# The second FFN's rows of three batches, added by GpSimd's adding transfers in place of fetches and VectorE sums

## The chip, the cores and the metric

The kernel runs on one core of one Trainium2 chip. The metric is the device time of one execution in microseconds (us), the median of several runs. PE is TensorE, ACT is ScalarE, DVE is VectorE, POOL is GpSimd; SyncE issues most DMA transfers from its queue, SPq.

## What is computed

`x` has 4 batches of 512 tokens with 256 channels. Four layers are added to it in turn. The change touches how the result of the last one is added.

```python
x = x + attention_a(layernorm(x))      # 16 heads of 16, 4 key groups, causal
x = x + ffn(layernorm(x))              # 8 experts, the best 2 of each token
x = x + attention_b(layernorm(x))      # linear attention over 4 memory banks
x = x + ffn(layernorm(x))              # the same experts again

def ffn(x):
    probs = softmax(x @ Wr);  w, idx = top_k(probs, 2);  w = w / sum(w)
    y_e = (silu(x @ Wg[e]) * (x @ Wu[e])) @ Wd[e]
    return sum over the 2 chosen e of w_e * y_e
```

## The kernel before

`xall` [128, 16, 256] holds x in SBUF, four tiles of 128 tokens for each of the 4 batches (`b`), and every layer adds to it there. The two FFNs (`f` = 0 and 1) route each token to two experts. The normed rows are scattered by expert into `xs[f]` in HBM (`scatter`). The experts then work through 39 tiles (`TILES`) of 128 rows each; a tile is a pass of steps `load` (SyncE), `xT`, `gate_up`, `hidden`, `down` (TensorE, each followed by ScalarE or VectorE work) and a last `down` on GpSimd, an indirect DMA that scatters the weighted 128x256 results `yo` into `ys[f]` in HBM (L1876), two rows (k = 0, 1) for each token. The tiles are sorted so that those before number 31 (`MIXED`) have all rows of batches 0 to 2, and the last eight, 31 to 38, finish batch 3. VectorE writes `yo` in four buffers (`NYO` = 4): `down` of tile j there waits until the scatter of tile j - 4 has landed.

When the last four tiles that a batch needs have landed (27 to 30 for batches 0 to 2, 35 to 38 for batch 3), `combine` (L455) brings its rows back, in one of two ways.
- A batch in `JOINED` (L194) is fetched: for each half h, SyncE issues a `fetch` of two transfers (k = 0, 1) of 256 KB from `ys` into `fetched`, which lies in the memory of `kbd` (L913; the profile names it `kbd<-ys`), and VectorE does a `join`, two sums of 128x512 into `xall` (L1734, L1735). There are two buffers, so the third fetched batch of the list waits for the first one's joins.
- A batch that is not in it gets two steps `add` on GpSimd, k = 0 and 1 (L1870): each one transfer of 512 KB with `accum_op=ALU.add` that adds the k rows of the whole batch straight to `xall`. The k = 1 transfer waits on GpSimd until the k = 0 one has landed. Before the change these are batches 1 to 3 of the first FFN.

After that SyncE writes the batch out, two `store` steps of 256 KB (L919), and at the end waits for all eight.

**The order on the engines** is made when the program is built. `plan_work` (L516) lists each step with its engine, a rank, a planned duration, a planned time from issue to landing (`lands`), and what it waits for; `Work.order` (L141) goes through time and, for the step that can start first, lets a step of lower rank on that engine go ahead if it can start hardly later (`PATIENCE`). Each engine then issues its steps in exactly that order. Its planned numbers are the program's own and not measured. Ranks at the end are `last + 3j + 6` for `down` of tile j and `last + 78 + b` for `combine` of batch b. The planner's entries for the steps of `combine` and the stores are these.

```python
# combine, not in JOINED (k = 0, 1); rows: the last four scatters the batch needs
w.add(POOL, rank + 0.1 * k, 1.4, "add", f, b, k, after=rows + [(POOL, "add", f, b, 0)] * k,
      behind=[(POOL, "pow", 1, 0)], lands=8.0)
# in JOINED
w.add(SP, rank + 0.1 * k, 0.75, "fetch", f, b, k, after=rows + ([(DVE, "join", *JOINED[n - 2], 1)] if n >= 2 else [])
      + [(SP, "fetch", f, b, 0)] * k, lands=3.3)
w.add(DVE, rank, 1.34, "join", f, b, h, after=[(SP, "fetch", f, b, h)], behind=[(DVE, "join", f, b, 0)] * h)
```

Of the kernel before, what the change touches and what calls it, by code (L numbers as in the profile page):

```python
# [17 lines left out]
B, S, D = 4, 512, 256  # L18
# [28 lines left out]
TILES = 2 * B * S // P + NE - 1  # L47
# [143 lines left out]

JOINED = [(0, 0)] + [(1, b) for b in range(B)]  # L194


def tiles_with(b):
# [4 lines left out]
def spread(lo, hi, n):  # L202

    return iter([lo + (hi - lo) * (k + 0.5) / n for k in range(n)])


PE, ACTE, DVE, POOL, SP = "PE", "ACT", "DVE", "POOL", "SP"
# [130 lines left out]
def back(w, b, ranks):  # L338

    r = lambda: next(ranks)  # L340
    m = M_BANKS if b < B - 1 else TAIL_BANKS
    w.add(PE, r(), 0.45, "outT", b, after=[(DVE, "normalize", b, g) for g in range(NG)], banks=m, emptied=(ACTE, "outT", b))
    w.add(ACTE, r(), 0.92, "outT", b, after=[(PE, "outT", b)] + [(PE, "project", b - 1, 1)] * (b > 0))
    for n in range(2):
        w.add(PE, r(), 1.05, "project", b, n, after=[(ACTE, "outT", b), (ACTE, "out_weights")], behind=[(PE, "project", b, 0)] * n, banks=m,
              emptied=(DVE, "project", b, n))
        w.add(DVE, r(), 0.6, "project", b, n, after=[(PE, "project", b, n), (ACTE, "f_apply", b, 1)]
              + [(applies(b, NT - 1), "f_apply", b, NT - 1)])
# [9 lines left out]
def norm(w, s, b, ranks, banks):  # L358


    r = lambda: next(ranks)
    last = before(s, b)
    for n in range(2):
        src = ([(DVE, "project", b, n)], [(DVE, "join", 0, b, n) if (0, b) in JOINED else (POOL, "add", 0, b, 1)],
               [(DVE, "mem_out", b, 2 * n), (DVE, "mem_out", b, 2 * n + 1)])[s]
        w.add(DVE, r(), 1.15, "stats", s, b, n, after=src + ([(POOL, "pow", *last), (DVE, "scale", *last)] if last else []))
    w.add(POOL, r(), 1.03, "pow", s, b, after=[(DVE, "stats", s, b, n) for n in range(2)]
          + ([(ACTE, "apply", *last, NT - 1)] if last else []))
    w.add(DVE, r(), 0.1, "scale", s, b, after=[(POOL, "pow", s, b)] + ([(ACTE, "apply", *last, NT - 1)] if last else []))
    if s == 1:  # L370
        old = [(PE, "turn", 1, b - 1, kc) for kc in range(KC) if b]
    else:
        old = [(POOL, "scatter", s // 2, b - 2, i, k) for i in range(NT) for k in range(2)] if b >= 2 else []
        if s == 2 and b < 2:
            old = [(POOL, "scatter", 0, b + 2, i, k) for i in range(NT) for k in range(2)]
    for i in range(NT):
        w.add(ACTE, r(), 0.49, "apply", s, b, i, after=[(DVE, "scale", s, b)] + old
              + [(ACTE, "apply", s, b, i - 1)] * (i > 0))
    if s != 1:
        w.add(SP, r(), 0.5, "copy", s, b, after=[(ACTE, "apply", s, b, NT - 1)], lands=2.5)  # L380
    for kc in range(KC):
        w.add(PE, r(), 0.44, "turn", s, b, kc, after=[(ACTE, "apply", s, b, NT - 1)], behind=[(PE, "turn", s, b, 0)] * kc, banks=banks,
              emptied=(ACTE, "turn", s, b, kc))
        w.add(ACTE, r(), 0.5, "turn", s, b, kc, after=[(PE, "turn", s, b, kc)]
              + ([(PE, "mq", b - 1, mc) for mc in range(KC) if b] if s == 1 else
                 [(PE, "router", last[0] // 2, last[1])] if last else []))
# [68 lines left out]
def combine(w, f, b, rank):  # L455

    done = tiles_with(b)
    rows = [(POOL, "down", f, j) for j in range(done - NYO, done)]
    n = JOINED.index((f, b)) if (f, b) in JOINED else None
    for k in range(2):  # L460
# [3 lines left out]
        else:  # L464

            w.add(SP, rank + 0.1 * k, 0.75, "fetch", f, b, k, after=rows + ([(DVE, "join", *JOINED[n - 2], 1)] if n >= 2 else [])
                  + [(SP, "fetch", f, b, 0)] * k, lands=3.3)
# [48 lines left out]
def plan_work():  # L516
    w = Work()
    unit = lambda u: UNIT * u
    w.add(SP, -999, 1.2, "load_x", 0, lands=2.6)
    w.add(SP, -998, 0.5, "load_x", 1, behind=[(SP, "load_x", 0)], lands=2.8)  # L520
    w.add(SP, -997, 0.5, "constants", behind=[(SP, "load_x", 1)], lands=5.2)
    w.add(SP, -996, 4.0, "load_late", behind=[(SP, "constants")], lands=11.0)
    w.add(SP, unit(2), 2.0, "load_experts", behind=[(SP, "place_keys", 0, NG - 1)], lands=20.0)
    w.add(ACTE, -600, 0.8, "constants", after=[(SP, "constants")], behind=[(ACTE, "f_apply", 0, 1)])
    w.add(POOL, -700, 0.7, "bias", after=[(SP, "constants")])
    w.add(ACTE, unit(20), 0.8, "out_weights", after=[(SP, "constants")], behind=[(ACTE, "queriesT", 0, 2)])
    w.add(DVE, -999, 3.0, "presets")
    w.add(DVE, -800, 0.3, "constants", after=[(SP, "constants"), (DVE, "presets")])
    w.add(DVE, -500, 0.15, "scales", after=[(SP, "constants")])
    w.add(DVE, -300, 0.35, "masks", after=[(SP, "constants")])  # L530
    w.add(POOL, -999, 6.4, "presets")
    w.add(POOL, -500, 1.2, "constants", after=[(DVE, "scales"), (POOL, "presets")])
    w.add(POOL, unit(6), 1.7, "late", after=[(SP, "load_late"), (POOL, "constants")])
    for k, time in enumerate((0.5, 2.6)):
        w.add(DVE, unit(16), time, ("bank_shift", "banks")[k], after=[((SP, "load_late"), (ACTE, "banks"))[k],
                                                                      (DVE, "queries", 0, 1)])
    w.add(ACTE, unit(16), 0.3, "banks", after=[(DVE, "bank_shift")])
    w.add(SP, unit(8), 8.0, "spare", after=[(POOL, "late"), (SP, "load_experts")])
    tail = unit(BU * B)
    for b in range(B):  # L540
        lo = unit(BU * (b - 1) + 2)
        front(w, b, spread(-900, -100, 64) if b == 0 else spread(lo, unit(BU * b - 5), 64))
        scores(w, b, unit)
        t0 = unit(BU * (b + 1) + NU + 1 + LAG)
        t1 = unit(BU * (b + 1) + (26 if b == B - 2 else 36))
        if b == B - 1:
            t0, t1 = tail, tail + 1
        back(w, b, spread(t0, t0 + 0.3 * (t1 - t0), 8))
        m = M_BANKS if b < B - 1 else TAIL_BANKS
        norm(w, 0, b, spread(t0 + 0.3 * (t1 - t0), t0 + 0.7 * (t1 - t0), 16), m)  # L550
        route(w, 0, b, spread(t0 + 0.7 * (t1 - t0), t1, 16), m)
    release(w, 0, 0, unit(BU * B - 2), M_BANKS)
    release(w, 0, 1, unit(BU * B + 2), M_BANKS)
    release(w, 0, 2, tail + 2, TAIL_BANKS)
    for j in range(TILES):
        rank = tail + 20 + 3 * j + 8 * max(0, j - MIXED)
        rest = (1, 2) if j < LEAD else (2, 3, 4) if j < STAGES[LAST][1] else (2, 3, 4, 7)
        tile(w, 0, j, rank, 3, {"X": rest, "G": (0, 1)[:1 + (j >= LEAD)], "H": rest, "Y": rest})
    start = tail + 20 + 3 * MIXED
    for b in range(B):  # L560
        combine(w, 0, b, start - 20 + b)
        t = start + TURN * b
        memory(w, b, t - 18, t, t + TURN)
        norm(w, 2, b, spread(t + TURN, t + TURN + 6, 16), (7,))
        route(w, 1, b, spread(t + TURN + 6, t + TURN + 12, 16), (7,))
    last = start + TURN * (B + 1)
    for n, (batches, _, _) in enumerate(STAGES):
        release(w, 1, n, start + TURN * batches + 13, (7,))
    for j in range(TILES):
        rest = (3, 4, 5, 6) if j < STAGES[LAST][1] else (3, 4, 5, 6, 7)  # L570
        tile(w, 1, j, last + 3 * j, 3, {"X": rest, "G": (1, 2), "H": rest, "Y": rest})
    for b in range(B):
        combine(w, 1, b, last + 2 * TILES + b)
        for h in range(2):
            w.add(SP, last + 2 * TILES + b + 0.5, 0.4, "store", b, h, after=[(DVE, "join", 1, b, h)], lands=2.8)
    return w


ORDER, PLACE = plan_work().order()

FIRST_PACK = {"ident": (P,), "wqkv": (KC, QKV), "bqkv": (QKV,), "nscale": (2, 2, HD), "turns": (2, NT, HD), "mask": (P,)}
# [9 lines left out]
def build(nc, x, first_pack, late_pack, norm_sums, experts, out):  # L591
# [4 lines left out]
    with ExitStack() as ctx:  # L596
# [215 lines left out]
        def combined(eng, f, b, halves=2):  # L812

            if (f, b) in JOINED:
                eng.wait_ge(joined, 2 * JOINED.index((f, b)) + halves)
            else:
                eng.wait_ge(added[b], 16 * 2 * sum((g, b) not in JOINED for g in range(f + 1)))

# [1138 lines left out]
```

## Time and profile before

| | |
|---|---|
| median of 3 runs | 535.22 us (531.47 to 540.63) |
| the profiled execution, whole | 536.22 us |
| its span, first to last instruction | 534.4 us |
| PE busy | 483.7 us (91%) |
| DVE busy | 373.3 us (70%) |
| POOL busy | 248.5 us (46%) |
| DMA, mean over the span | 114 GB/s |
| SyncE's DMA queue (q1) | 38.24 MB, 23.0% of 16 engines' span |
| GpSimd's DMA queue (q0) | 21.83 MB, 13.6% |
| mean granted TensorE clock | 0.965 |

Busy shares are means over stages that differ. The span starts with the first attention. The first FFN's tiles (matmuls of L1138) begin at 187 us and end before 305, the second attention is mixed in and follows, and the second FFN's tiles run from 407.7 to 518 us. The last 16 us hold no matmul. Times below are us from the span's start.

### The profile page before, as it was taken

To read this page: it belongs to the slowest core of one execution; us is meant where nothing else is said; L and a number is where in the kernel's file an instruction comes from. 1 tells how busy PE (TensorE), PEld (TensorE's weight loads), DVE (VectorE), ACT (ScalarE), POOL (GpSimd) and SP (SyncE) were. 2 spreads that over 40 slices of the span, in tenths; PEclk is the share of its full clock that TensorE was granted. 3 is DMA by queue.
4 is the path that set the end of the run, shared out by engine and by line. 5 is a ranking of instruction groups with operands and counts; after the bars stand their busy time and mean duration, and the time that the engine had idled before them with its cause. 6 is when DMAs were issued, how large, how long until landed. Compare 5 with 4: busy or idle time off the path is not lost.

```text
span 534.4 us, 10902 instructions
## 1 busy us (share of the span) xinstructions
PE 483.7 (91%) x3346; PEld 327.6 (61%) x3346; DVE 373.3 (70%) x1098; ACT 269.3 (50%) x642; POOL 248.5 (46%) x308
## 2 busy tenths in 40 slices
PE   5799899999999999989999979999979998999960
PEld 2335555665665666766777636675757776677740
DVE  4799989879999966664445647868868684344473
ACT  3578898877887784423333425524223532334320
POOL 5408519338850062373433555446473756233330
PEclk8789999999999999999999999999989999799995
DMA  8254510111120232454335392102151457233484
GB/s 278 114 198 206 165 35 8 56 41 61 61 84 19 84 129 78 122 187 140 95 113 158 76 191 41 37 34 81 41 155 43 141 158 209 80 101 107 161 295 165
DMA packets 43736, 60.77 MB, mean 114 GB/s; under 512 B 5856, under 2 KB 38240, under 8 KB 43040
## 3 DMA queue, kind: packets, MB, share of 16 engines
q1 hardware_dynamic: 33696, 38.24, 23.0%
q0 software_dynamic: 9984, 21.83, 13.6%
q8 instruction: 29, 0.48, 0.4%
q14 instruction: 27, 0.22, 0.1%
HBM read 28.89 MB, written 25.00 MB: 101 GB/s over the span
## 4 chain that ended last, share of the span: by engine, by line
PE 58%; DVE 10%; DMA 5%; issue 4%; ACT 2%; POOL 2%; SPq 1%; POOLq 0%; DVEq 0%; ACTq 0%
PE PS L1138 15%; PE PS L1155 10%; PE PS L1184 4%; PE PS L1025 3%; PE PS L1119 3%; PE PS L1147 3%; PE PS L1002 3%; PE PS L1193 3%; PE PS L1087 2%; PE PS L1201 2%; DMA ys<-yo,xin 2%; DVE smax L1477 2%; PE PS L1165 2%; PE PS L1076 2%; DMA kbd<-ys 2%
## 5 line engine op out<-in xcount | busy, mean ns | idle before, releaser
L1876 POOL DMA_INDIRECT ys<-yo,xin x78 | 75.4, 966 | 107.3 <-DVE yo L1698 97.6
L1138 PE MATMUL PS<-wexp,xTt 128*128 x312 | 106.8, 470 | 2.2 <-issue 1.3
L1477 DVE TENSOR_REDUCE smax<-PS 128x1 f32<-128x512 f32 (+3 forms) x176 | 102.3, 633 | 6.1 <-PE PS L1004 5.6
L1303 ACT ACTIVATE prob<-PS 128x512 f16<-128x512 f32 (+1 forms) x176 | 92.7, 562 | 20.1 <-PE PS L1027 18.2
L1861 POOL DMA_INDIRECT xs<-xn,pos x64 | 62.5, 977 | 57.9 <-DVE pos L1572 40.8
L1155 PE MATMUL PS<-wexp,hT 88*128 x312 | 81.3, 388 | 2.3 <-ACT hT L1353 2.1
L1138 PEld LDWEIGHTS PS<-wexp,xTt 128*128 128x128 f32 x312 | 55.6, 192 | 25.1 <-issue 5.2
L1685 DVE SCALAR_TENSOR_TENSOR sg<-th,PS 128x176 f32<-128x176 f32 x78 | 26.2, 336 | 61.6 <-ACT th L1347 61.3
L1347 ACT ACTIVATE th<-PS 128x176 f32<-128x176 f32 x78 | 24.7, 317 | 83.9 <-PE PS L1138 83.9
L1155 PEld LDWEIGHTS PS<-wexp,hT 88*128 88x128 f32 x312 | 55.9, 191 | 15.2 <-issue 4.2
L1025 PE MATMUL PS<-qT,kbd 128*128 128x512 f16 (+3 forms) x256 | 60.8, 300 | 2.2 <-ACT qT L1295 1.0
L1002 PE MATMUL PS<-kbd,qT 128*128 128x512 f16 (+1 forms) x176 | 60.3, 367 | 2.4 <-DVE smax L1477 1.7
L1698 DVE TENSOR_SCALAR yo<-PS,xin 128x256 f32<-128x256 f32 x78 | 37.4, 482 | 26.3 <-PE PS L1155 22.6
L1353 ACT ACTIVATE hT<-PS 88x256 f32<-88x256 f32 x78 | 29.5, 378 | 40.2 <-PE PS L1147 39.3
L1004 PE MATMUL PS<-mask_b,ident_b 128*128 128x128 bf16 (+2 forms) x176 | 43.2, 245 | 0.0
L1027 PE MATMUL PS<-ident_b,mask_b 128*128 128x128 bf16 (+2 forms) x176 | 42.8, 243 | 0.0
L1043 PEld LDWEIGHTS PS<-vaug,prob 128*128 128x128 f16 x640 | 32.8, 96 | 16.1 <-ACT prob L1303 3.0
L1043 PE MATMUL PS<-vaug,prob 128*128 128x17 f16 x640 | 38.6, 172 | 1.5 <-ACT prob L1303 1.3
L1184 PE MATMUL PS<-late_rows,qT 128*128 128x512 f32 x64 | 33.3, 625 | 5.1 <-DVE qa L1724 4.7
L1883 POOL TENSOR_TENSOR qa<-qa 128x256 f32<-128x256 f32 x32 | 23.2, 756 | 23.5 <-DVE qa L1724 23.4
L1147 PE MATMUL PS<-first_rows,hf 128*88 128x128 f32 x156 | 30.2, 275 | 3.9 <-DVE hf L1689 3.6
L1341 ACT ACTIVATE xTt<-PS 128x256 f32<-128x256 f32 x78 | 26.4, 382 | 10.1 <-PE PS L1119 9.7
(210 smaller groups left out, 836.7 us busy)
## 6 DMA issues: line engine op xcount, KB each, us to landing
xin<-xs SPq DMA_DIRECT2D x78, 129.0 KB, 2.1
kbd<-ys SPq DMA_DIRECT2D x20, 256.0 KB, 4.3
wexp<-in_experts SPq DMA_DIRECT2D x4, 1216.0 KB, 9.1
xs<-zeros SPq DMA_DIRECT2D x32, 129.0 KB
xn<-xn SPq DMA_DIRECT2D x8, 512.0 KB, 3.3
xall<-ys POOLq DMA_DIRECT2D x6, 512.0 KB, 6.8
out<-xall SPq DMA_DIRECT2D x8, 256.0 KB, 2.7
kbd<-kT SPq DMA_DIRECT2D x60, 32.0 KB, 1.9
```

What stands on the lines that cost most here:

```text
L1002: pe.matmul(o, qT1[:, b % 2, g, i * P:(i + 1) * P], kbd[:, g, r0:r0 + nr, 0:w], start=True, stop=False, skip_group_check=True)
L1004: pe.matmul(o[:, :, i * P:w], ident_b[:], mask_b[:].unsqueeze(1).to_broadcast([P, nr, P]), start=False, stop=True, skip_group_check=True). ...
L1025: pe.matmul(o[:, k], kbd[:, g, r0 + k, j * P:(j + 1) * P], qT2[:, g % 2, j * P:S], start=(k == 0), stop=False, skip_group_check=True)
L1043: mm = pe.matmul(o[:, i, r0 + k], prob[:, u % NPR, k * w + (i - j) * P:k * w + (i - j + 1) * P], vaug[:, b, j, g], start=(n == 0 and k == ...
L1138: mm = pe.matmul(PS[:, bank, 0:2 * FI], xTt[:, j % NXT, kc * P:(kc + 1) * P], wexp[:, bass.ds(expert[f, j], 1), kc * 2 * FI:(kc + 1) * 2 * FI]
L1147: mm = pe.transpose(PS[0:FH, bank, c * P:(c + 1) * P], hf[:, j % 2, c * FH:(c + 1) * FH], ident_f)
L1155: mm = pe.matmul(PS[:, bank, 0:D], hT[:, j % 2, c * P:(c + 1) * P], wexp[0:FH, bass.ds(expert[f, j], 1), DOWN + c * D:DOWN + (c + 1) * D] ...
L1184: pe.matmul(PS[:, bank], sig[:, b % 2, kc, i * P:(i + 1) * P], late["mem"][:, kc], start=True, stop=True).then_inc(filled[bank], 1)
L1303: act.activation(prob[:, u % NPR, 0:nr * w], PS[:, bank, 0:nr * w], ACT.Exp, scale=ATT_SCALE)\
L1477: dve.tensor_reduce(smax[:, i, REP * g + r0:REP * g + r0 + nr], PS[:, bank, 0:nr * w].rearrange("p (r w) -> p r w", r=nr), AX.X, ALU.max). ...
L1861: pool.indirect_dma_start(xs[f], bass.IndirectOffsetOnAxis(pos[:, f, b, i, k:k + 1], axis=0), xn[:, b % 2, i, k], None).then_inc(scattered ...
L1876: pool.indirect_dma_start(ys[f], bass.IndirectOffsetOnAxis(xin[:, j % NXIN, D + 1:D + 2].bitcast(I32), axis=0), yo[:, j % NYO], None).then ...
```

## The change

The list `JOINED` loses batches 0, 1 and 2 of the second FFN. They are then added by GpSimd's transfers like batches 1 to 3 of the first. Batch 0 of the first FFN and batch 3 of the second stay fetched; batch 3 becomes the list's second, so it has a buffer of its own and no fetch waits for a join. The planner is told that a store of the three batches waits for the k = 1 add. `combined` (L812), `fetch`, `join` and `add` in the engines' programs read the same list and need no edit.

```diff
--- before.py
+++ after.py
@@ -191,7 +191,7 @@
 
 
 
-JOINED = [(0, 0)] + [(1, b) for b in range(B)]
+JOINED = [(0, 0), (1, B - 1)]
 
 
 def tiles_with(b):
@@ -572,7 +572,8 @@
     for b in range(B):
         combine(w, 1, b, last + 2 * TILES + b)
         for h in range(2):
-            w.add(SP, last + 2 * TILES + b + 0.5, 0.4, "store", b, h, after=[(DVE, "join", 1, b, h)], lands=2.8)
+            w.add(SP, last + 2 * TILES + b + 0.5, 0.4, "store", b, h, after=[(DVE, "join", 1, b, h) if (1, b) in JOINED else (POOL, "add", 1, b, 1)],
+                  lands=2.8)
     return w
```

## Rows read from the trace of the kernel before

**Rows 1.** The page: the span.

```profile
span 534.4 us, 10902 instructions
```

**Rows 2.** Chain of waits, 515 to 534 us: start, us, what.

```profile
519.18 4.25 DMA ys<-yo,xin
...
523.57 0.36 SPq L913
...
524.49 0.47 SPq L919
...
525.53 4.39 DMA kbd<-ys
...
529.95 0.70 DVE xall L1734
```

**Rows 3.** Timeline of SyncE's queue, 490 us on: start, us, queue, line, operation.

```profile
502.40 2.61 SPq L913 DMA_DIRECT2D kbd<-ys  x4
505.20 0.36 SPq L903 DMA_DIRECT2D xin<-xs  x1
505.73 1.94 SPq L913 DMA_DIRECT2D kbd<-ys  x4
```

**Rows 4.** Timeline of GpSimd, 490 us on: also idle before [releaser].

```profile
503.43 0.96 POOL L1876 DMA_INDIRECT ys<-yo,xin  x1 [0.30 <-issue]
...
519.18 0.96 POOL L1876 DMA_INDIRECT ys<-yo,xin  x1 [0.30 <-issue]
```

**Rows 5.** Timeline of VectorE, 490 us on.

```profile
510.97 0.48 DVE L1698 TENSOR_SCALAR yo<-PS,xin 128x256 f32<-128x256 f32 x1
...
514.64 0.48 DVE L1698 TENSOR_SCALAR yo<-PS,xin 128x256 f32<-128x256 f32 x1
...
517.93 0.48 DVE L1698 TENSOR_SCALAR yo<-PS,xin 128x256 f32<-128x256 f32 x1 [1.41 <-PE PS L1155]
```

**Rows 6.** Timeline of TensorE: `down` of tiles 34, 35 and 38.

```profile
506.90 1.13 PE L1155 MATMUL PS<-wexp,hT 88*128 x4
...
510.45 1.03 PE L1155 MATMUL PS<-wexp,hT 88*128 x4
...
516.77 1.12 PE L1155 MATMUL PS<-wexp,hT 88*128 x4 [0.56 <-ACT hT L1353]
```

**Rows 7.** Timeline of GpSimd, 300 to 315 us (first FFN's adds).

```profile
301.63 2.75 POOL L1870 DMA_DIRECT2D xall<-ys  x2
304.68 1.09 POOL L1876 DMA_INDIRECT ys<-yo,xin  x1 [0.30 <-issue]
...
309.63 4.08 POOL L1870 DMA_DIRECT2D xall<-ys  x3
```

**Rows 8.** Lines L1870 and L1876 in three short stretches: issues, us to landing.

```profile
L1870 POOL DMA_DIRECT2D xall<-ys x2: 1400/1632/1865, 301.6 to 302.5; - x2
DMA to landing us min/median/max: 5.8/6.7/7.6
...
L1870 POOL DMA_DIRECT2D xall<-ys x3: 1441/1741/1947, 309.6 to 312.0; - x3
DMA to landing us min/median/max: 6.0/7.8/9.0
...
L1876 POOL DMA_INDIRECT ys<-yo,xin x1: 1025/1025/1025, 306.1 to 306.1; - x1
DMA to landing us min/median/max: 4.7/4.7/4.7
```

**Rows 9.** Stretches: busy us of PE, PEld, DVE, ACT, POOL; PEclk, DMA share, GB/s.

```profile
304.00:309.00 5.00, 4.06 (x20) 2.60 (x19) 0.97 (x2) 2.79 (x6) 3.79 (x5) 1.00 1.20 181
309.00:311.00 2.00, 2.00 (x6) 0.76 (x4) 0.08 (x1) 1.23 (x2) 2.00 (x3) 1.00 1.03 319
505.00:507.00 2.00, 1.88 (x11) 1.18 (x9) 0.92 (x3) 0.84 (x4) 0.96 (x1) 1.00 1.06 364
```

**Rows 10.** Line L1876, all 78 scatters: us to landing.

```profile
DMA to landing us min/median/max: 2.4/2.6/6.2
```

## The prediction

> **What bounds the kernel now.** I read the page first: one core, span 534.4 us [rows 1]. The edit can only act on the last 32 us, so I then read the end of the chain of waits backwards [rows 2], and from 502 us on the timelines of the queues and engines that the edit touches: SyncE's queue [rows 3], GpSimd [rows 4], VectorE [rows 5] and TensorE [rows 6]. The chain ends in batch 3, which the edit leaves alone. The last `down` scatter (tile 38) is issued at 519.18 and is followed until 523.43. Then come the four fetches of batch 3, in two pairs with one store between them (523.57 to 525.53). The last lands at 529.92, two sums follow, and the last store ends the span. From 523.57 to 534.4 this is 10.8 us. Everything that the edit removes belongs to batches 0 to 2. It matters only as far as it is ahead of that chain: in SyncE's queue, in the DMA engines, or in VectorE and GpSimd ahead of tiles 34 to 38.
>
> **Removed: twelve fetches.** Six pairs, of which the first four, eight transfers, start at 502.40 and 505.73 [rows 3]. Their cost on the path is small. The load of tile 38 waited behind the first four and is issued at 505.20 instead of about 502.4. TensorE does not idle for it, so I give it nothing. Their traffic also slows the scatters: 2.6 us is the usual landing, 6.2 the worst, 4.25 the last one [rows 2, 10]. At most 1.7 us can come back there, if nothing takes the place of this traffic.
>
> **Removed: twelve sums on VectorE, 0.69 us each, 8.3 us.** They keep tile 34's `yo` from about 508.1 to 510.97 and tile 35's from 511.48, where its matmuls end, to 514.64 [rows 5, 6]. But tiles 36 to 38 are paced by TensorE: tile 38's matmuls run 516.77 to 517.89 and its `yo` follows at 517.93 with no sum before it. GpSimd could then issue at 518.41 + 0.27 = 518.68 and issues at 519.18 [rows 4], because four scatters stand in a row, 1.26 us each. So 0.5 us hangs on the sums, and perhaps 0.7 more on `gate_up` 38, which with an earlier load can run ahead of `down` 36 (a `down` pass is 1.03 to 1.13 us, of which the planner's order gives back a part). Together at most 1.2 us, if GpSimd is free.
>
> **Added: six adding transfers of 512 KB on GpSimd's queue.** The trace has the same operation for the first FFN. Two take 2.75 us of GpSimd, three take 4.08 [rows 7]. The three are issued from 309.6 to 312.0; the first lands after 6.0, at 315.6, the third after 9.0, at 321.0, so they land 2.7 us apart, as the two before them do (307.4 and 310.1) [rows 8]. So n of them back to back land 3.3 + 2.7n us after the first issue. While adds flow the DMA engines are full (share 1.20) at 181 GB/s. With the plain fetches they are full too (1.06) and move 364 [rows 9]. An added byte costs twice a fetched one. The pages state another price, which stands among the rivals.
>
> The second fact is the order in that queue. A scatter issued at 306.08, behind two adds that landed at 307.4 and 310.1, landed after 4.7, at 310.8 [rows 8]; all four scatters went through at 309 to 311, at 319 GB/s, once the adds were through [rows 9]. So a `down` scatter behind an add waits for its bytes.
>
> **Where the planner puts them.** I use its costs for the order alone. Row 30 is due in the plan just after `down` 32 has gone, so the three k=0 adds, whose rank is lower than that of any later tile, go behind it and before `down` 33. It holds a k=1 add ready 8 us after its k=0 add. That is 490.84, 492.24 and 493.64 in its count. `down` 33, 34 and 35 are due earlier (at latest 489.2), but 36, 37 and 38, at 491.7 to 494.3, are not. So all three k=1 adds should stand ahead of the last three `down` scatters, on GpSimd and in its DMA queue.
>
> Step by step: GpSimd ends `down` 32 at 504.39, plus the 0.30 it takes between issues gives 504.7 for the first add. The k=0 adds are issued until 508.8, and land at 510.7, 513.4 and 516.1. `down` 33 goes at 509, 34 at 510.3, 35 at 512.3. The k=1 adds follow from 513.5; the third waits until 516.1, and behind it on GpSimd wait `down` 36 to 38, issued at 518.3, 519.6 and 520.8. VectorE's `yo` 37 needs row 33 landed, about 516.4 against 515.7 when it is due, which the wait on GpSimd hides. So issue is 1.6 us later than 519.18, but it is not what ends last. The DMA queue then holds six adds, 3.3 + 6 x 2.7 = 19.5 us, and six scatters of 0.13 MB at 319 GB/s, 2.5 us: the last lands at 504.7 + 19.5 + 2.5 = 526.7, where before it was 523.4. That is **+3.3**. The two stores of batch 0, due at about 520, share the engines: 0.52 MB at 364 GB/s is 1.4 us if added in full, nothing if it fits between the adds. I take nothing, as the adds' low rate leaves room, and keep 1.4 for the range.
>
> **Moved: the stores.** A store of batches 0 to 2 now waits for its k=1 add. In the plan batch 0's two stores come before the first pair of batch 3's fetches and four more between the pairs, as the second pair is held until the first has landed. Today one stands there [rows 2]. Three more, 0.47 + 0.05 us each, put the second pair off by 1.6 us. If the bytes decide and not the issue (three stores, 0.79 MB at 364 GB/s), it is 2.2; I take **+1.6**, because the row has this wait in issue time. SyncE itself waits nowhere else: adds 1 and 2 stand ahead of the last scatters in the DMA queue and have landed by then.
>
> **Sum.** +3.3 + 1.6 = +4.9 us. The profiled execution took 536.22 us, its span of 534.4 and 1.8 around it; it becomes 541.1. It stands 1.0 above the median shown, 535.22, so I predict **540.1**.
>
> **Rivals.**
> *The adds are cheap* (538.4). If their bytes are no limit, only GpSimd's issue counts: the last scatter at 520.8, +1.6, landing as long as now, and +1.6 for the stores: +3.2. The rows' 2.7 us between landings, in both groups, speaks against it. The Trainium skill (DMA: Bandwidth & Descriptors, section "Anatomy of one DMA — SWDGE (gpsimd) path") states 2.0 us plus bytes at 436 GB/s for a transfer of this path. By that an add of 512 KB would take 1.2 us of data, and the sum would be this rival's.
> *The last scatters go first* (535.4). If the planner or my hand count of it differs by the 0.9 us between 490.84 and 491.7, `down` 36 to 38 pass the k=1 adds. Then batch 3 comes up to 2.9 us earlier (1.2 and 1.7 above), but the k=1 adds start at about 519.3 and land 11.4 later, at 530.7; two stores, 1.0, a landing of 2.1 and the usual end of 0.9 make 534.7 against 534.4. So nothing is gained even here; with the adds at half price it could reach 532.
> *Slower by over 2%* (546 and more). The place is the same DMA queue: if in this traffic an add takes 3.7 us instead of 2.7, six of them add 6 us to the 4.9. From 3.7 on it decides. For it: the stores and TensorE's last loads were not beside the adds in the rows. Against it: only one load and two stores can be.
>
> **Chances.** The forecast's mechanism 0.66, with its own range from 538.4 (the DMA queue's part down to GpSimd's 1.6) to 542.1 (3.3 + 1.4 + 2.2 = +6.9). Cheap adds 0.12, last scatters first 0.13, slower 0.09. The range goes from the second rival, 535, to the edge of the third, 546. A change under 2% (10.7 us) is about what a measurement of this kernel cannot tell from none: the runs shown differ by 1.7%. Faster by over 2% would need more than the sums, the traffic and the queue hold together: 0.01. Slower by over 2%: 0.08. Within: 0.91.
>
> **What the changed profile should show.** GpSimd's timeline: three adds after the seventh-last scatter, three more before the third-last; a wait of GpSimd for the third k=0 add near 516. Adds landing 2.7 us apart at a DMA share near 1.2 and 180 to 190 GB/s from 507 to 525. The last scatter issued at about 521 and landing about 6 us later, near 526.7. Four stores between the two pairs of fetches. VectorE idle behind TensorE, tile 35's `yo` at 511.5. I am wrong if scatters land within 3 us of issue between the adds, if the adds come closer than 2 us, or if `down` 38 stands before the second group.

## The result and the profile after

The changed kernel took 546.23 us (median of 4 runs, 541.48 to 547.7), the kernel before, in the runs beside it, 537.92 (531.47 to 541.13). The ratio is 1.0171, 95% interval 1.0124 to 1.0219: 1.7% slower. A second timing in five rounds on another chip, where the kernel before takes 580 us, gave 1.010 (1.0064 to 1.0135). The forecast was 540.1, a slowdown of 4.9 us, with a range up to 546.0. Its mechanism is what the profile shows; two of its sizes were too small, and the time fell just outside the range.

The profiled execution has a span of 545.9 us against 534.4. The page of the changed kernel, GpSimd's queue q0 beside SyncE's q1:

```profile
span 545.9 us, 10878 instructions
...
PE 485.2 (89%) x3346; PEld 328.2 (60%) x3346; DVE 366.0 (67%) x1086; ACT 269.2 (49%) x642; POOL 256.9 (47%) x314
...
q1 hardware_dynamic: 30432, 35.09, 21.5%
q0 software_dynamic: 13152, 24.98, 17.2%
```

VectorE lost its twelve sums (373.3 to 366.0 us busy), and 3.15 MB moved from q1 to q0 (38.24 to 35.09, 21.83 to 24.98). GpSimd's timeline, which answers to [rows 4] and shows the operations of [rows 7] in the new place (start, us, engine, line, operation; in brackets the idle time before):

```profile
507.90 0.96 POOL L1877 DMA_INDIRECT ys<-yo,xin  x1 [0.31 <-issue]
508.86 4.06 POOL L1871 DMA_DIRECT2D xall<-ys  x3
513.23 1.07 POOL L1877 DMA_INDIRECT ys<-yo,xin  x1 [0.30 <-DVE yo L1699]
514.60 1.01 POOL L1877 DMA_INDIRECT ys<-yo,xin  x1 [0.30 <-issue]
516.85 0.95 POOL L1877 DMA_INDIRECT ys<-yo,xin  x1 [1.24 <-DVE yo L1699]
517.80 4.09 POOL L1871 DMA_DIRECT2D xall<-ys  x3
522.20 1.06 POOL L1877 DMA_INDIRECT ys<-yo,xin  x1 [0.30 <-issue]
523.57 1.01 POOL L1877 DMA_INDIRECT ys<-yo,xin  x1 [0.30 <-issue]
524.89 0.96 POOL L1877 DMA_INDIRECT ys<-yo,xin  x1 [0.31 <-issue]
```

The order is the one that was worked out: three adds behind the scatter of tile 32, three more behind that of tile 35, and the last three scatters behind those. The chain of waits at the end, which answers to [rows 2] (start, us, what):

```profile
524.89 7.25 DMA ys<-yo,xin
...
532.22 0.37 SPq L914
...
532.62 0.47 SPq L914
...
533.14 0.47 SPq L920
...
533.65 0.47 SPq L920
...
534.16 0.54 SPq L920
...
534.75 0.99 SPq L920
...
535.91 0.89 SPq L914
...
536.85 4.31 DMA kbd<-ys
...
541.18 0.70 DVE xall L1735
```

The last scatter is issued at 524.89 and is followed for 7.25 us (before: 4.25). Then four stores (L920) stand between the two pairs of fetches (L914), where one stood. Batch 0's two stores go earlier, beside the last scatters. In SyncE's timeline they are this line:

```profile
525.19 1.84 SPq L920 DMA_DIRECT2D out<-xall  x2
```

**How to compare.** The two profiles differ before they reach the change: the scatter of tile 32, ahead of which every engine runs the same instructions in the same order, is issued at 507.90 and in before at 503.43. This start moves from run to run; in the four other profiles below that were taken where before needs some 540 us, the same code reached it between 501.5 and 504.0. In this pair the gap had grown in small steps to 1.9 us at a scatter issued at 449.80 (447.86 in before), and five scatters on it was 4.5 (468.80 and 464.32). Between them lie these stretches of before, and then of the changed kernel (columns as in [rows 9]; a granted clock of 1.00 is 2.4 GHz, 0.50 is 1.2 GHz):

```profile
450.00:460.00 10.00, 7.73 (x22) 4.60 (x21) 2.62 (x7) 1.99 (x6) 3.15 (x4) 0.66 0.52 157
460.00:470.00 10.00, 10.00 (x49) 7.25 (x49) 4.15 (x11) 3.98 (x13) 2.88 (x3) 1.00 0.21 65
```

```profile
450.00:460.00 10.00, 6.22 (x20) 3.90 (x19) 2.43 (x6) 1.23 (x4) 4.29 (x5) 0.74 0.59 157
460.00:470.00 10.00, 9.87 (x35) 6.38 (x35) 2.99 (x8) 3.04 (x9) 1.26 (x2) 0.75 0.17 41
```

TensorE was idle for longer in the first stretch, and the lower clock reached into the second. In the changed kernel once more (next section) both stretches ran at 1.00, and tile 32's scatter went at 504.03. So most of the late start comes and goes from one execution of the same kernel to the next. All runs are therefore compared by their **tail**, from the issue of tile 32's scatter to the end of the span, cut where the last scatter has landed.

```
kernel                  tile 32   last scatter landed   rest   tail
before                   503.43         20.0            11.0   31.0
before, once more        549.85         20.6            10.9   31.6
after                    507.90         24.2            13.8   38.0
after, once more         504.03         24.5            13.7   38.2
after, once more         546.67         23.8            13.3   37.1
```

Before: 534.4 - 503.43 = 31.0, cut at 519.18 + 4.25 - 503.43 = 20.0 [rows 2, 4]. After: 545.9 - 507.90 = 38.0, cut at 524.89 + 7.25 - 507.90 = 24.2. The difference is 7.0 us in the first pair. On the other chip it is 5.6. Both agree with the timings: 7.0 of 537.9 is 1.3%, 5.6 of 580 is 1.0%, each inside its interval. (The ratio's own middle on the first chip, 1.7%, would be 9 us; that the 2 us beyond the tail are the spread ahead of the change fits the late start above, but is shown for this one pair of profiles only.)

### The profile page after: what moved, and what is told of

Read it like the earlier page. It is cut to its first block, busy times and chain, and to the rows that moved or that the text cites. A ratio compares the mean times of both kernels' runs of the same rounds, so it can differ in the third digit from the quotient of the medians.

```text
span 545.9 us, 10878 instructions
## 1 busy us (share of the span) xinstructions
PE 485.2 (89%) x3346; PEld 328.2 (60%) x3346; DVE 366.0 (67%) x1086; ACT 269.2 (49%) x642; POOL 256.9 (47%) x314
## 3 DMA queue, kind: packets, MB, share of 16 engines
q1 hardware_dynamic: 30432, 35.09, 21.5%
q0 software_dynamic: 13152, 24.98, 17.2%
## 4 chain that ended last, share of the span: by engine, by line
PE 56%; DVE 9%; DMA 5%; POOL 4%; issue 4%; ACT 3%; SPq 1%; POOLq 0%; DVEq 0%; ACTq 0%
PE PS L1139 15%; PE PS L1156 10%; PE PS L1026 3%; PE PS L1185 3%; PE PS L1120 3%; PE PS L1148 3%; POOL xs L1862 3%; PE PS L1003 3%; DMA ys<-yo,xin 3%; PE PS L1194 2%; DVE smax L1478 2%; PE PS L1088 2%; PE PS L1202 2%; PE PS L1077 2%; PE PS L1166 2%
```

## The experiments

### The changed kernel once more

> The changed kernel once more, unedited, to see how far its last part repeats. Measure for all runs: the tail, from the issue of tile 32's scatter (the last one ahead of the first adds) to the end of the span, which is 31.0 us before the change and 38.0 after. The profile after already showed two parts: the last scatter lands 24.2 us after tile 32's issue (before: 20.0), and from there to the end it takes 13.8 us (before: 11.0). Both theories expect the tail at 38.0 within 0.5 us, whatever the whole span is; if it moves by more than 1 us, single looks at the tail prove nothing.

Unedited. Span 542.2 us, tail 38.2: the last scatter landed after 24.5, the rest took 13.7. The whole differs from the first profile by 3.7 us, the tail by 0.2, so single profiles can be compared by their tail.

### The kernel before once more

> The kernel before once more, unedited: how far its last part repeats. Expected: the last scatter landed 20.0 us after tile 32's issue and a tail of 31.0, each within 0.7 us, whatever the whole span is.

Unedited. Span 581.4, tail 31.6 (20.6 and 10.9). A chip on which the whole takes 9% longer has nearly the same tail. Before repeats within 0.7 us, and the three profiles of the changed kernel put the last landing at 23.8 to 24.5 and the tail at 37.1 to 38.2. Most kernels below have one profile each, so a difference of a microsecond or less is a hint and no more.

### Stores of batches 1 and 2 behind batch 3's fetches

```diff
-                  lands=2.8)
+                  lands=2.8, behind=[(SP, "fetch", 1, B - 1, 1)] if 1 <= b < B - 1 else [])
```

> The four stores of batches 1 and 2 are issued behind the second pair of batch 3's fetches and no longer between the pairs. Theory (issue order): the second pair goes 2.7 us earlier, relative to the first pair, so the tail falls from 38.0 to about 35.3. Rival (bytes: the DMA engines have the same MB to move before the end): the tail stays at 37.5 or more. The landing of the last scatter stays at 24.2 under both.

Tail 36.2: landing 24.1, rest 12.1. SyncE's queue:

```profile
518.64 2.26 SPq L920 DMA_DIRECT2D out<-xall  x2
525.95 1.92 SPq L914 DMA_DIRECT2D kbd<-ys  x4
527.91 6.71 SPq L920 DMA_DIRECT2D out<-xall  x6
```

All four fetches are issued within 1.92 us. The theory wanted a tail 2.7 us shorter and got 1.8; the rest fell by 1.6 of the 2.8 us. From the last scatter's landing to the issue of the last fetch it is 1.5 us (4.7 in the change), so 3.2 us of issue went away. But that fetch lands 5.38 us after its issue and not 4.31, and from its landing (532.78) to the end it is 5.2 us and not 4.7: the four stores' bytes now follow close behind. So 1.5 us came back as bytes. Issue order is the larger part of this term, and neither rival is right alone.

### All six stores of batches 0 to 2 behind the fetches

```diff
-                  lands=2.8)
+                  lands=2.8, behind=[(SP, "fetch", 1, B - 1, 1)] if 0 <= b < B - 1 else [])
```

> All six stores of batches 0 to 2 go behind the second pair of fetches, the two of batch 0 too, whose bytes moved together with the last three scatters. Theory: the last scatter lands up to 1.3 us earlier than 24.2 after tile 32's issue, and the tail is about 34.3, 1 us under the kernel with four late stores. Rival (these two stores only fill gaps and cost nothing, as the prediction took): landing stays at 24.2 and the tail equals the other kernel's.

The last scatter landed after 23.15, 0.9 earlier than in the run above and 1.1 earlier than in the change. That is what batch 0's two stores cost when they run beside the last scatters, from one profile; against the three of the changed kernel (23.8 to 24.5) it is 0.7 to 1.3. It is close to the 23.3 of the prediction's sum, in which they were given nothing. The tail did not follow: 36.1, rest 13.0. With six stores left for the end, the last fetch landed 6.3 us after the first was issued, as in before, but the end came 6.6 us after that and not 4.5. The expectation of 34.3 failed by this.

### Transfers that copy in place of adding

```diff
-     ... k=2)[k], accum_op=ALU.add)\
+     ... k=2)[k], accum_op=ALU.add if f == 0 else ALU.bypass)\
```

> The second FFN's transfers on GpSimd's queue copy and do not add (the output lacks x and one of the two rows there); place, size and waits are those of the changed kernel. Theory (the adding transfers take twice the DMA time, and the scatters wait behind them in their queue): each takes about 1.4 us instead of 2.7, the last scatter lands 20 to 21 us after tile 32's issue instead of 24.2, and the tail falls to about 34. Rival (GpSimd's issue order and its wait for the first group decide, not the rate of the adds): landing at 23.5 or later and a tail of 37.5 or more.

The output lacks x and one of the two rows. The last scatter landed after 20.8 (24.2 with adds), the rest took 13.8 and the tail 34.6. Three copies hold GpSimd for 2.36 us, three adds for 4.06. Stretches of the copy kernel, and then of the changed one (start and end, us; busy us of PE, PEld, DVE, ACT and POOL; granted clock, DMA share, GB/s):

```profile
506.00:510.00 4.00, 4.00 (x22) 2.99 (x21) 1.16 (x3) 2.02 (x7) 2.96 (x4) 1.00 0.83 254
515.00:519.00 4.00, 1.49 (x7) 0.78 (x5) 0.97 (x2) 0.38 (x1) 3.09 (x5) 1.00 0.88 244
```

```profile
512.00:518.00 6.00, 6.00 (x28) 4.26 (x27) 2.49 (x7) 2.04 (x7) 4.16 (x5) 1.00 1.23 194
522.00:528.00 6.00, 0.00 (x0) 0.00 (x0) 0.00 (x0) 0.00 (x0) 3.04 (x3) 0.58 1.21 192
```

With adds the engines are full (1.23, 1.21) at 194 and 192 GB/s. With copies of the same size in the same places they are not full (0.83, 0.88) at 254 and 244. So 3.5 of the 4.2 us in the landing of the last scatter go away with the adding. The order of steps on GpSimd, which is the same here, costs what remains, at most 0.8, against a spread of 0.6 of this figure in before.

Two things change with the adding, and the run alone does not part them: the rate, and the time for which GpSimd is held (the last scatter is issued 15.2 us after tile 32's, 17.0 with adds). That the rate decides is read from the changed kernel's trace: from 512 to 529 its queue q0 kept the DMA engines at a share of 1.03 or more in every microsecond, so an earlier issue would have had to wait. A third thing changes too. The adds move in packets of about 1 KB (194 packets, 0.20 MB, from 515 to 516), the copies mostly in packets of about 4 KB (107 packets, 0.39 MB, from 507 to 508). The packet size alone does not make a byte dear: SyncE's transfers in packets of 1 KB moved 367 GB/s at a share of 1.05 (374 packets, 0.37 MB, from 534 to 535 in the changed kernel).

### The second adds behind the last scatter

```diff
-                  behind=[(POOL, "pow", 1, 0)], lands=8.0)
+                  behind=[(POOL, "pow", 1, 0)] + [(POOL, "down", 1, TILES - 1)] * (f * k), lands=8.0)
```

> The second group of adds (k = 1) is issued behind the last scatter; this is the prediction's rival 'the last scatters go first'. The last scatter should land about 18.5 us after tile 32's issue (24.2 in the changed kernel). The adds then go at about 16 and land until 27.4. Theory of the prediction (SyncE's transfers and the adds share the engines): batch 3's fetches move beside the adds, and the end is set by the stores behind the last add, a tail of about 33. Rival, from the profile after, where two stores issued at 525.2 moved no byte until the adds were through at 529: the plain transfers wait for the adds, the fetches land at about 31, and the tail is 36 to 37.

The last scatter landed after 17.3 us, 2.7 earlier than in before, and the tail was still 37.7. The chain of waits:

```profile
564.98 2.40 DMA ys<-yo,xin
...
567.47 0.38 SPq L914
...
567.90 0.50 SPq L914
...
568.56 1.12 SPq L914
...
569.72 9.90 DMA kbd<-ys
```

The four fetches are issued at once, but the last lands 9.90 us after its issue (4.39 in before). Two stretches of this kernel, the first with adds alone, the second with adds and plain transfers together:

```profile
568.00:570.00 2.00, 0.00 (x0) 0.00 (x0) 0.00 (x0) 0.00 (x0) 2.00 (x2) 0.50 1.01 124
574.00:580.00 6.00, 0.00 (x0) 0.00 (x0) 1.73 (x3) 0.00 (x0) 0.00 (x0) 0.50 1.19 231
```

Together they moved 231 GB/s at a share of 1.19. By queue, microsecond by microsecond, from 574 to 580 q0 and q1 moved 0.11 to 0.16 and 0.06 to 0.13 MB each; neither had its own rate of 0.19 or 0.36. Ahead of that, no byte of q1 moved until 570, 2.5 us after the first fetch was issued. The prediction's rival "the last scatters go first", priced at no change, is wrong by 6 us: it let the fetches pass the adds freely. The expectation's rival said 36 to 37, by a strict wait that the run does not show; it is a shared rate after a late start. Against before the rest is 9.4 us longer (20.4): 5.5 are this landing, and 3.7 follow it, since all eight stores are issued from 575.50 on and end the span 8.2 us after the last fetch has landed (4.5 in before).

### Two batches added, one fetched

```diff
-JOINED = [(0, 0), (1, B - 1)]
+JOINED = [(0, 0), (1, 2), (1, 3)]
```

> Batches 0 and 1 are added, batch 2 fetched: four adds and not six. If each add costs its 2.7 us in the queue ahead of the last scatters, the last scatter lands about 19.7 to 21 us after tile 32's issue, and with four stores between the pairs of fetches the tail is 33.5 to 35, between the 31.0 of before and the 38.0 of the change. Rival (the harm is a threshold, GpSimd's wait for the third add): landing at 20 or less and a tail of 31 to 32 less the stores' part, 33.8 at most.

Landing after 21.0, rest 13.8, tail 34.7. GpSimd here waits for the landing of an add:

```profile
565.27 1.43 POOL L1871 DMA_DIRECT2D xall<-ys  x1
568.23 1.31 POOL L1871 DMA_DIRECT2D xall<-ys  x1 [1.52 <-DMA xall<-ys]
569.84 1.06 POOL L1877 DMA_INDIRECT ys<-yo,xin  x1 [0.30 <-issue]
```

The tail lies between before and after, where the theory had it. It does not tell the theory from the threshold cleanly, since the landing of 21.0 is only 0.4 from the second before.

### One batch added, two fetched at once

```diff
-JOINED = [(0, 0), (1, B - 1)]
+JOINED = [(0, 0), (1, 1), (1, 2), (1, 3)]
```

> Only batch 0 is added; batches 1 and 2 are fetched at once, neither waiting for a buffer. Two adds end long before the last scatters, and no fetch runs beside them any more: the last scatter lands 18 to 18.5 us after its mark (before: 20.0). With two stores between the pairs of fetches and not one (+0.5) the tail is about 29.8 against 31.0 before, 0.2% faster, which five rounds may not tell from nothing. Rival (any add in that queue costs): a tail above 31.5 and a slower kernel.

Slower than before by 1.0% (1.0105, 1.0051 to 1.0159); tail 33.2 (21.5 and 11.7). The theory fell here. I had asked only what two adds do to the last scatters. What they do to the fetches beside them shows on VectorE:

```profile
552.67 0.69 DVE L1736 TENSOR_TENSOR xall<-xall,kbd 128x512 f32<-128x512 f32 x1
555.55 0.69 DVE L1735 TENSOR_TENSOR xall<-xall,kbd 128x512 f32<-128x512 f32 x1 [2.18 <-DMA kbd<-ys]
556.27 0.69 DVE L1736 TENSOR_TENSOR xall<-xall,kbd 128x512 f32<-128x512 f32 x1
556.88 0.33 DVE L1686 SCALAR_TENSOR_TENSOR sg<-th,PS 128x176 f32<-128x176 f32 x1
557.25 0.34 DVE L1690 TENSOR_TENSOR hf<-sg,PS 128x176 f32<-128x176 f32 x1
557.50 0.48 DVE L1699 TENSOR_SCALAR yo<-PS,xin 128x256 f32<-128x256 f32 x1
```

```profile
553.00:557.00 4.00, 2.97 (x12) 1.77 (x10) 1.78 (x4) 0.79 (x3) 0.00 (x0) 1.00 1.16 229
```

While the add and the fetches share the engines at 229 GB/s, the second `join` waits 2.18 us for its fetch (0.32 in before). The gate of tile 36 and tile 34's `yo` stand behind it in VectorE's order, so TensorE gets the one and GpSimd the other late: GpSimd idles 6.59 us before tile 34's scatter (5.02 in before), and the last scatter is issued 19.1 us after tile 32's, not 15.75.

### The same with the stores ahead

```diff
+                  behind=[(SP, "store", 0, h) for h in range(2)] if (f, b) == (1, B - 1) else [])
```

> As with one batch added, but the six stores of batches 0 to 2 all stand ahead of batch 3's first fetch, with nothing between the pairs. Theory: from the landing of the last scatter to the end 10.5 us instead of 11.0 (before) or 11.5, a tail of about 29, and 0.3 to 0.4% faster than before. Rival (the stores ahead wait for the add and hold up the fetches): a tail of 31 or more.

1.0052 (1.0009 to 1.0094), slower than before and perhaps 0.5% better than the kernel above (the intervals overlap). The expected gain did not come. Its one profile is of its longest execution (592.65 us, median 587.37). The rest there is the expected 10.5 us and the tail 32.9, but an execution so far from the median settles neither figure, and they stay open.

### The changed kernel timed again

> The changed kernel, timed in five rounds. If the change acts in the tail alone (38.0 to 38.2 us against 31.0 in three looks), it is 7.1 us slower than before, a ratio of 1.013 on a chip where before takes about 537 us. Rival (the change also slows what stands ahead of it, as the 4.5 us by which tile 32's scatter came later in the first pair of profiles would say): 1.02 or more.

1.010 (1.0064 to 1.0135) and a tail of 37.1 against 31.6: 5.6 us, which explains the ratio. The rival, 1.02 or more, is out.

### Four buffers and no adds

```diff
-                        if n >= 2:
-                            sp.wait_ge(joined, 2 * (n - 1))
+                        if n >= 4:
+                            sp.wait_ge(joined, 2 * (n - 3))
+        def landing(n, k, h):
+            if n < 2:
+                return fetched[:, n, k, 2 * h:2 * h + 2]
+            return xn[:, n - 2, 2 * h:2 * h + 2, k, 0:D]
+     behind=... + [(DVE, "down", 1, TILES - 1)] * (f == 1 and b == 2)
```

The edit is shortened: the planner's entry, the semaphores and the joins use four buffers likewise.

> The kernel before with all fetches of batches 0 to 2 issued at once, into four buffers instead of two, batch 2's joins behind the last yo, and all six of their stores ahead of batch 3's first fetch; no adds. Theory (the last scatters suffer from the transfers beside them, 4.3 us to landing in before, 2.4 where nothing ran): the last scatter lands 18 to 18.5 us after tile 32's issue, the tail is about 29 and the kernel 0.3 to 0.4% faster than before. Rival (the fetches only press closer together and the joins hold VectorE): a tail of 31 or more.

1.0015 (0.9978 to 1.0052): no difference. Tail 31.3. The rest became 10.3 and the last scatter lands 3.27 us after issue instead of 4.25, as hoped, but it is issued 17.8 us after tile 32's and not 15.75: the joins of batches 0 and 1 wait for fetches that now share the engines with more of their kind, and hold VectorE's `yo` (tile 35's scatter goes 14.0 us after tile 32's, 12.0 in before). No version beats the kernel before: the three variants that were timed had ratios of 1.0015 to 1.0105, and all others have longer tails.

## Why the prediction was wrong in size and right in kind

**Where it acts, and the order.** Right. The planner put the adds where the hand count had them; the k = 0 adds landed 6.1, 7.9 and 9.7 us after issue ([rows 8] has 6.0 to 9.0), and the DMA engines ran at 1.23 and 194 GB/s from 512 to 518 ([rows 9]: 1.20 and 181). Tile 37's `yo` waited for row 33 as foreseen, 1.65 us, until 520.68, hidden because GpSimd was held by the second group of adds until 521.89. The wait of GpSimd for the third k = 0 add was hardly there: 0.37 us in the changed kernel once more, none that this profile shows.

**"+3.3" for the DMA queue.** Right without the stores: 23.3 us to the last landing was the sum, 23.15 was measured where no store ran beside it. One step that failed is the sentence on batch 0's two stores, "I take nothing, as the adds' low rate leaves room". A low rate was not room: the DMA share was 1.24, all of it GpSimd's queue, while the stores waited. They cost 1.1 us (24.2 against 23.15; 0.7 to 1.3 over the three profiles), near the 1.4 that had been kept for the range only.

```profile
525.00:529.00 4.00, 0.00 (x0) 0.00 (x0) 0.00 (x0) 0.00 (x0) 0.85 (x1) 0.50 1.24 208
530.00:532.00 2.00, 0.00 (x0) 0.00 (x0) 0.00 (x0) 0.00 (x0) 0.00 (x0) 0.50 0.72 258
```

The two stores are issued at 525.19 and after, and land 6.2 and 7.2 us later. Until 529 they moved nothing. From 529 to 532 they moved their 0.5 MB, just when the third add of the second group and the last scatters had to get through, and this is where the scatters lost time.

**"+1.6" for the stores between the fetches.** Right in kind, 1.2 short: the rest grew from 11.0 to 13.8. The sentence took 0.47 + 0.05 us for each of three more stores. In the chain above the four take 0.47, 0.47, 0.54 and 0.99 and the next fetch 0.89, where [rows 2] has 0.47 and 0.36. The first pair and the second are 3.69 us apart (532.22 to 535.91), 1.56 in before: +2.1; the longer fetch issue adds 0.5. A price from a row with five transfers in a row did not hold for seven: the first four issues take 0.37 to 0.47, the fifth 0.54, the sixth 0.99, the seventh 0.89. The second profile (0.53, 0.85, 0.99) and the copy kernel (0.55, 0.73, 1.06) show the same. That the transfers already in the queue cause it is argued, not shown. The copy kernel has the same 13.8, so this does not come from the adds. Nor was it issue alone, as "the row has this wait in issue time" took it: with the stores moved away, 1.5 of 3.2 us came back as bytes.

**The sum.** 3.1 (23.15 - 20.0) + 1.1 + 2.8 = 7.0, the 7.0 of the tail; 4.9 was predicted. Even the mechanism's own upper bound, +6.9, was just too low.

**The range.** Its upper edge, 546.0, added all bounds and stopped where the third rival began, but left no room for the start of the tail, which alone moves by several microseconds. The runs shown of before had said so (531 to 541). The measured time is 6.1 us above 540.1. Of these, 2.1 are the two sizes above, 2.7 are the kernel before itself, which took 537.92 in the runs beside and not the 535.22 that the forecast started from, and 1.3 are the rest of the difference of medians, ahead of the tail. That 546.23 lies in the band of the third rival is no point for it, since its mechanism did not happen.

**The gains that were looked for** were real and lay where no end depended on them. Tile 34's `yo` came 2.9 us closer to tile 32's scatter (512.53 - 507.90 = 4.6 against 7.5 [rows 4, 5]), and the freed GpSimd slot went to the adds. With the adds moved away, the last scatter landed 2.7 us earlier than in before, about the 2.9 that was estimated (3.3 against before once more).

**The rivals.** "The adds are cheap" (+3.2) is what the copy kernel measured for copies, +3.6 in the tail: right for copies, wrong for adds. By the fit in the Trainium skill (DMA: Bandwidth & Descriptors, section "Anatomy of one DMA — SWDGE (gpsimd) path") a transfer of 512 KB takes an estimated 3.2 us. The quickest copy here landed after 3.9 us and the quickest add after 5.8 (first add of the changed kernel once more), so the fit is near for the copy and far off for the add. "The last scatters go first" had the right 2.7 us of gain and missed that adds and fetches slow each other. The slower rival did not happen: adds landed 2.6 to 3.0 us apart within each group and not 3.7.

## What to carry to other kernels

Moving a sum from an engine with slack into the transfer frees nothing, and here the transfer that adds filled the DMA engines at about half the rate of a plain one, so that what was queued behind it, and the transfers beside it, came late. Before moving work into a DMA queue, list what is issued to that queue later and what shares the engines at that time, and price both. Align profiles at the last unchanged instruction before comparing them; the whole span can differ by more than the change.

## What the runs showed of the hardware

Adding transfers of 512 KB from HBM to SBUF ran at 192 to 194 GB/s with the DMA engines full (share 1.21 to 1.23), in packets of about 1 KB. Plain ones on the same queue ran at 244 to 254 at a mean share of 0.83 to 0.88, in packets of about 4 KB, with single microseconds at 389 GB/s and 0.98. Plain ones on SyncE's queue, in packets of 1 KB, reached 367 at 1.05.

Beside adding transfers, plain transfers of the other queue started late: two stores issued from 525.19 moved nothing until 529, four fetches issued from 567.47 nothing until 570. With nothing beside it, a fetch issued at 532.22 had moved bytes before 534. The adding is not needed for all of this: beside copies, stores issued at 517.82 moved nothing until 520. Later both queues moved together. From 574 to 580, with adds and plain transfers, they moved 231 GB/s in sum, each below its own rate.

The first four transfers issued in a row from SyncE's queue took 0.36 to 0.47 us of issue each, the sixth and seventh 0.70 to 1.10 in the changed kernel's three profiles and in the copy kernel's.
